# Row maxima of all batches on two banks, the first key rows with a bank and tiles of their own, and the rotations of batches 1 and 2 by ScalarE and GpSimd

## What is computed

```python
# layer 0, per batch
h = layernorm(x) * (1 + ca) + sa                # sa, ca, ga, ... from silu(c) @ wmod
qkv = h @ w_qkv.T                               # 16 heads, head size 8
q, k = rope(q), rope(k)                         # t * cos + rotated(t) * sin
x = x + ga * (softmax(q @ k.T) @ v) @ w_out.T   # 16 heads, 512 x 512 scores each
h = layernorm(x) * (1 + cb) + sb
x = x + gb * top2_of_8_experts(h)               # silu(h w0) * (h w1), then wo
# layer 1, per batch
x = x + ga * gated_unit(layernorm(x) ...)       # hidden, q/k similarity over channels, output
x = x + gb * one_expert(layernorm(x) ...)       # 128 -> 512 -> 128, gelu
```

## Time and profile before

| | |
|---|---|
| median of 3 runs | 981.61 us (981.26 to 983.02) |
| the profiled execution's own time | 982.85 us |
| its span, first to last instruction | 981.0 us |
| mean granted TensorE clock | 0.916 of full speed |
| TensorE busy | 831.7 us (85%) |
| VectorE busy | 696.9 us (71%) |
| ScalarE busy | 579.7 us (59%) |
| GpSimd busy | 461.6 us (47%) |

### The profile page before, as it was taken

The page is one execution under the profiler, slowest core; times in us unless marked ns, Lnnn a source line. Parts: engine busy times, 40 slices in busy tenths (PEclk is TensorE's granted clock), DMA queues, the critical chain, the costliest instruction groups (busy, mean ns, idle before and its releaser), DMA issues. The chain is left out here.

```text
span 981.0 us, 15587 instructions
## 1 busy us (share of the span) xinstructions
PE 831.7 (85%) x4972; PEld 449.9 (46%) x4972; DVE 696.9 (71%) x1454; ACT 579.7 (59%) x923; POOL 461.6 (47%) x607
## 2 busy tenths in 40 slices
PE   4788888998789978998899989988899888799586
PEld 3222232544245515654464544634564557376353
DVE  6888786688678756788678658847877435577574
ACT  2256676575567466866686668546857864443252
POOL 0152144025458535573747367383645763663201
PEclk9558889999899979999999989989999999889688
DMA  7524344354824354446073613680156045010001
GB/s 207 164 92 99 73 99 164 86 161 130 208 52 148 122 165 92 113 123 192 25 214 95 202 28 114 182 247 17 42 179 198 25 147 180 24 39 19 1 12 38
DMA packets 97063, 110.77 MB, mean 113 GB/s; under 512 B 14191, under 2 KB 76783, under 8 KB 95616
## 3 DMA queue, kind: packets, MB, share of 16 engines
q1 hardware_dynamic: 92954, 102.06, 36.6%
q0 software_dynamic: 3584, 7.35, 2.6%
q10 hardware_dynamic: 444, 0.36, 0.1%
HBM read 84.06 MB, written 26.26 MB: 112 GB/s over the span
## 5 line engine op out<-in xcount | busy, mean ns | idle before, releaser
L1459 ACT ACTIVATE probs<-scores 128x1024 f32<-128x1024 f32 x256 | 262.0, 1024 | 116.0 <-PE scores L1077 84.8
L1772 DVE TENSOR_REDUCE negmax<-scores_for_max 128x2 f32<-128x1024 f32 x192 | 234.3, 1220 | 59.0 <-PE scores_for_max L1052 45.8
L1087 PE MATMUL weighted_values<-probs,vaug 128*32 128x512 f32 x1024 | 147.6, 653 | 1.1 <-ACT probs L1459 1.1
L1149 PE MATMUL expert_units<-xt,ring 128*128 128x128 f32 x840 | 122.7, 289 | 13.4 <-DVE mu L1949 5.6
L1077 PE MATMUL scores<-qs,ks 51*128 51x512 bf16 x512 | 106.0, 407 | 32.3 <-ACT probs L1459 27.9
L1149 PEld LDWEIGHTS expert_units<-xt,ring 128*128 128x128 f32 x840 | 105.2, 195 | 56.3 <-issue 47.6
L1052 PE MATMUL scores_for_max<-ks,qs 48*128 48x512 bf16 x384 | 76.8, 396 | 15.8 <-DVE negmax L1772 11.3
L2222 POOL DMA_INDIRECT xs_d<-xbn,rowpos x56 | 55.6, 994 | 50.2 <-DVE rowpos L1905 35.4
L2233 POOL DMA_INDIRECT y<-ys_d,rowpos x56 | 55.4, 989 | 37.9 <-DMA ys_d<-slot_rows 21.4
L1077 PEld LDWEIGHTS scores<-qs,ks 51*128 51x128 bf16 x512 | 25.5, 94 | 103.2 <-ACT probs L1459 64.2
L1768 DVE TENSOR_REDUCE negmax<-scores_for_max 128x1 f32<-128x512 f32 x86 | 56.4, 682 | 7.5 <-PE scores_for_max L1046 3.6
(11 more groups left out here) (325 smaller groups left out, 1666.3 us busy)
## 6 DMA issues: line engine op xcount, KB each, us to landing
ring<-in_experts SPq DMA_DIRECT2D x113, 384.0 KB, 5.2
slot_rows<-xs_d SPq DMA_DIRECT2D x7, 960.0 KB
parts_d<-parts SPq DMA_DIRECT2D x15, 384.0 KB, 2.6
qs<-parts_d SPq DMA_DIRECT2D x14, 384.0 KB
ks<-parts_d SPq DMA_DIRECT2D x14, 384.0 KB
ys_d<-slot_rows SPq DMA_DIRECT2D x21, 256.0 KB
w<-in_L_ffn_w SPq DMA_DIRECT2D x16, 256.0 KB
parts_d<-parts SPq DMA_DIRECT2D x15, 256.0 KB, 2.9
```

The costliest lines, as they stand in the source:

```text
L1087: last = nc.tensor.matmul(pv[32 * j:32 * j + 32, :], vaug[:, kt, PAIRS * (j // 2) + GP * g + j % 2, :], probs[:, kt % 2, j % 2, j // 2, :] ...
L1149: last = nc.tensor.matmul(dst[:, at], ring[:, q % RING, j, first + f * P:first + (f + 1) * P], xt[:, q % 2, at], start=True, stop=True)
L1459: nc.scalar.activation(probs[:, kt % 2, j, :, :].rearrange("p m s -> p (m s)"), se[:, :], ACT.Exp)\
L1772: V.tensor_reduce(negmax[:, g % 2, :, n], sm[:, :].rearrange("p (m s) -> p m s", m=2), AX, ALU.max, negate=True)\
```

## The change

1. The three banks of batches 0 and 1 go. All batches take the pair of banks and one reduction of 1024 columns. Only the first group of batch 0 alternates between the pair `sm` and the pair `se`, which no exponential uses yet.
2. In batch 0 the k projection has its own bank (`m0`, shared_ab), and its rotation, sum and remainder have tiles of their own (`uz`, `u2`, `nt3`), so that it waits for nothing of q. The modulation products that used `m0` go to `wp`. Several VectorE steps of the start wait until the last part of k is written.
3. `p_store` is a step for each part, sent when that part is written, and `p_stack` a step for q and one for k.
4. In batches 1 and 2 (`COPIED`) VectorE doesn't rotate. ScalarE copies the projection out of PSUM into `uz` and, with the halves exchanged, into `u2` (step `turn`, 3 ACTIVATEs), and GpSimd multiplies by `cosT` and `sinT` and subtracts (3 operations in place of its 1).
5. The whole slot table is new.

```diff
-EARLY = 2
+COPIED = (1, 2)
...
-        def max_unit(b, g, n, m):
-            return 2 * GROUPS * GP * NT * b + 2 * (GP * NT * g + n) + m
-
-        def max_unit_bank(u):
-            return (sm[:, 0:512], sm[:, 512:1024], wp[:, :])[u % 3]
+        def max_bank(b, g, n):
+
+            return se if b == 0 and g == 0 and n % 2 else sm
...
+        def proj_bank(b, n):
+            return m0 if (b, n) == (0, 1) else m1
+
+        def turned(b, n):
+
+            return (uz, u2, nt3) if (b, n) == (0, 1) else (rot1, rot2, rem)
...
-                if b < EARLY:
-                    for m in range(2):
-                        at, u = slice(HALF * m, HALF * m + STACK), max_unit(b, g, n, m)
-                        after(pe, "a_max", 0, u - 2)
-                        nc.tensor.matmul(max_unit_bank(u), qs[at, b % 2, p, t * P:(t + 1) * P], ks[at, b % 2, p, :],
-                                         start=True, stop=True).then_inc(sig["a_smf"], 1)
-                    return
-                after(pe, "a_max", b, 8 * g + n)
+                if b == 0 and g == 0:
+                    if n == 1:
+                        pe.wait_ge(s_m1, SM_COPIED)
+                    after(pe, "a_max", b, max(n - 1, 0))
+                else:
+                    after(pe, "a_max", b, 8 * g + n)
...
+            def turn(b, n):
+                if b not in COPIED:
+                    return
+                after(act, "p_proj", b, n + 1)
+                after(act, "p_sum", b, n)
+                nc.scalar.activation(uz[:, :], m1[:, :], ACT.Copy)
+                nc.scalar.activation(u2[0:HALF, :], m1[HALF:P, :], ACT.Copy)
+                nc.scalar.activation(u2[HALF:P, :], m1[0:HALF, :], ACT.Copy).then_inc(sig["p_rot"], 1)
...
             def mod_second(b, part):
 
                 if b == 0 and part == 0:
+                    after(dve, "p_part2", b, 2)
...
             def rot(b, n, k):
+                if b in COPIED:
+                    return
...
+                if b in COPIED:
+                    pool.wait_ge(s_rope, 16 * N_ROPE)
+                    first = 4 * COPIED.index(b) + 2 * n
+                    G.tensor_tensor(uz[:, :], uz[:, :], cosT[:, :], ALU.mult).then_inc(sig["p_mul"], 1)
+                    G.tensor_tensor(u2[:, :], u2[:, :], sinT[:, :], ALU.mult).then_inc(sig["p_mul"], 1)
+                    pool.wait_ge(sig["p_mul"], first + 2)
+                    G.tensor_tensor(rem[:, :], uz[:, :], u2[:, :], ALU.subtract).then_inc(sig["p_sum"], 1)
+                    return
...
-        ("P", "xT"): dict(pe=(86, 137, 160, 278, 389, 512, 671, 929)),
+        ("P", "xT"): dict(pe=(86, 153, 178, 278, 386, 513, 659, 902)),
```

More of the change, by code:

```diff
@@ L829, in p_stack @@
[L829 to L841 removed]
+                n = k if which else PARTS - 1 - k
```

468 lines of the change are left out of this document (232 added, 236 removed), and 118 rows, old and new, of the table SLOTS.

## The result

The changed kernel takes 992.33 us (median of 3 runs, 988.69 to 1000.0) where the kernel before takes 981.61: ratio 1.0117, 95% interval 1.0062 to 1.0171. It is slower by 10.7 us; the forecast was 4.9 us slower. The profiled execution is the longest of the three, with 1000.0 us and a span of 997.9; it took 7.7 us more than the median, so part of what stands in its trace is that execution's own.

A forecast was written before the change was run, and what follows sets the result against it. TensorE was held to bound the kernel from 165.5 us on, with no engine always full before; the change acts on the first 165 us. -2.8 + 3 + 5.1 - 0.4 = +4.9 us, by the median 986.5 us; range 974 to 992 us.

The forecast's parts named there:

- The pace: Attention units at full clock: reductions 1.71 us apart with 0.49 us idle for the refill, in place of 1.51 us.
- P of batch 1: Preparation of batch 1, moved behind the first maxima on TensorE, between exponentials: 6.4 us at half clock, costed at +3 us.
- rival c: First 165 us: a further clock loss or a full ScalarE makes it slower, 992 us; chance 0.11 together with late stack.
- The first reduction starts at about 35.4 us: 2.8 us earlier: Start of batch 0: shorter VectorE chain and batch 1's work moved behind the maxima, 35.4 in place of 38.18 us.
- The stack doesn't hold it: Start of batch 0: the stack DMAs of k land by 34.2 us, before the first reduction, with 1.2 us cover.
- One pair of banks: +5.1 us: Row maxima of batches 0 and 1 share one pair: 0.20 us a unit at full clock, bounds 0 to 31 us.
- Rotations "at nothing": Batches 1 and 2: VectorE loses 8.2 us of products, ScalarE gains 12 copies hidden in the refills; costed at nothing.
- theory C: Expectation set for Run 4: VectorE's freed 8.2 us were worth their time, 995 to 1000 us.
- 3.2 early: First exponential of batch 0: 2.8 us from the start and 0.4 us from no longer standing behind a projection.
- 3 + 0.8 + 1.6: Batch 0 losses: 3 us for batch 1's preparation, then bank-pair losses of 0.8 from 69.9 us and 1.6 from 104 us.
- The new slot table also reshuffles later batches ... I cost that at nothing: Order of later batches: moved by at most some 30 places of 1,250; nothing in the sum, put into the range.
- the sign of being wrong: From 165 us on: the prediction is wrong if that time changes by more than the start did.

The follow-up runs named there:

- run 6: Changed kernel with its start mended in three places (small constants behind v, first group sent ahead, gated weights behind the first partial maxima): 970.58 us, ratio 1.0096.
- run 5: Changed kernel again, unaltered, on the chip of the next three experiments: 972.35 us, ratio 1.0123 to the kernel before.
- run 12: Changed kernel with the old order from about 840 us on and the start mended in its three places: 976.62 us, ratio 1.0132.
- run 9: Changed kernel in its own order up to about 840 us, from there in the order of the kernel before: 979.3 us, ratio 1.0172.
- run 18: Changed kernel with the start mended in three places and the old order of the steps behind the transposes of step C of batch 7: 1000.29 us, ratio 1.0215.
- run 17: Changed kernel again, unaltered, beside the kernel with both ends mended: 1007.09 us, ratio 1.0278 to the kernel before.
- run 10: Kernel before in its own order up to about 840 us, from there in the changed kernel's order: 971.42 us, ratio 1.0087.
- run 1: Kernel before, own order, with the row maxima of batches 0 and 1 on one pair of banks instead of three single banks: 975.95 us, ratio 1.0168.
- run 8: Kernel before, own order, row maxima on one pair of banks, but on two pairs in turn in batch 0's first group: 972.55 us, ratio 1.0122.
- run 7: Changed kernel, in its order, with the row maxima of batches 0 and 1 on three single banks again: 971.27 us, ratio 1.0115.
- Run 4: Changed kernel with the rotations of batches 1 and 2 on VectorE again: 976.53 us, ratio 1.0179.
- run 2: Changed kernel in its own order up to about 167 us, from there in the order of the kernel before: 978.93 us, ratio 1.0188.
- run 13: Kernel before, unaltered, run for its trace: 978.27 us, ratio 0.998.
- run 16: Kernel before with the changed kernel's order of the last 60 us alone: 985.19 us, ratio 1.0033.
- run 3: Kernel before, own code and order up to batch 1's last row maximum, from there in the changed kernel's order: 972.27 us, ratio 1.0121.
- run 11: Kernel before with the changed kernel's order only between about 167 and 840 us: 978.24 us, ratio 1.0153.
- run 15: Changed kernel with the old order of the last 60 us alone: 997.45 us, ratio 1.0156.
- run 14: Changed kernel with the old order from about 840 us on for TensorE, VectorE and ScalarE, but its own on GpSimd: 1004.1 us, ratio 1.0192.

## Why the prediction was wrong

**What held.** The pace: 1.72 us a unit with 0.49 us of refill, and the last exponential of batch 0 at 120.24 us ("about 120 us"; the terms themselves give 118.9). The 3 us for P of batch 1 were not tested alone. That the early clock would cost more (rival c) is wrong for the first profiled run, which has more of the full clock up to 104 us than before. The measured 992.33 us is that rival's 992, by luck: up to 104 us the clock was not lost, and no run tested for a full ScalarE.

**"The first reduction starts at about 35.4 us: 2.8 us earlier".** It came at 38.14. The length of VectorE's chain was right (9.85 us for 9.7); the step failed because it took the start of that chain and the landing of the stack from the order of before. "The stack doesn't hold it", with 1.2 us of cover, is the sentence that fell: k lands 6 us after its issue, behind two large transfers that the changed code sends first, and the small constants ahead of v cost 2.3 us. Mended, the reduction is at 35.53 us, so the size was right for a kernel that does not have these waits. What it is worth at the end stays open: 1.8 us (run 6 to 5) and 2.7 us (run 12 to 9) by medians within the noise, with the lead gone by 110 us in both pairs of traces, and 2.9 us kept at 200 us in the third pair (run 18 to 17).

**"One pair of banks: +5.1 us".** In the old order it is about twice that: 1.0122, some 11 us, with 4.9 us at the end of batch 0 and 7 to 8 at 150 us. In the new order taking the pair away gives 1.1 us in the total, within the noise, and 2.4 to 2.8 us up to 155 us, before a stretch at a lower clock. So the price depends on the order: between exponentials a refill costs 0.2 us, as the term had it; maxima one behind another leave TensorE idle for 1.1 to 1.4 us each, and the clock is lower besides (run 10). The rule of the Trainium skill that the prediction weighed (Perfetto Trace Analysis, Optimizing Tensor Performance (Matmuls): independent groups rotate through banks) is borne out in the old order (runs 1 and 8); in the new one (run 7) the trace agrees with it up to 155 us, and the total doesn't show it. The term should have counted how many maxima stand bare; it used one share for all 64.

**Rotations "at nothing".** Not shown either way. Run 4, without the move, has the number of theory C, and is 7.1 us behind run 5 from 90 us on, a part of it by the clock. So the move may be worth some us, which the sum didn't have.

Errors of opposite sign nearly met by the end of batch 0: at the first exponential 0.9 us late where 3.2 early was forecast, and from there to the last exponential of batch 0 a loss of 2.6 us where the terms had 5.4 (3 + 0.8 + 1.6). Together 3.5 us late, 2.2 by the terms. That this came out near is luck.

**"The new slot table also reshuffles later batches ... I cost that at nothing".** This is the step that failed and that carries the number. Behind batch 1 lie 10.9 of the 16.9 us of the first pair of traces, and 15.2 of the 24.6 of the second (the first changed trace is 7.7 us above its median, so there the share behind batch 1 is uncertain). The term was nothing, with no reason but the number of places; and the sign of being wrong that the prediction named, a time from 165 us on that changes by more than the start did, came true. From the last exponential of batch 1 to the end of the trace, over all traces (us):

| order behind 167 us | chips where the kernel before takes 960 to 963 | chips where it takes 978 to 982 |
|---|---|---|
| old | 769.8, 770.1, 770.8 (runs 1, 2, 8) | 791.7, 788.6 (before, run 13) |
| old, with the new end | 769.9 (run 10, from 840 us) | 787.5 (run 16, last 60 us) |
| new | 772.4, 774.3, 770.4, 774.4, 769.9 (runs 5, 6, 7, 3, 4) | 802.6, 803.8 (changed, run 17) |
| new, with the old end | 779.5, 777.3, 779.3 (runs 9, 12, 11, from 840 us) | 797.6, 799.9 (runs 15, 18, last 60 us), 801.9 (run 14, from 840 us but for GpSimd) |

So the term at nothing measures -1 to 5 us on chips of the first kind and 11 to 15 (new against the order of before) on the kind on which the forecast stood. What is shown of it: about 5 us in the last 60 us, where the order of 11 steps on TensorE is the cause behind the new middle (from output 6 to output 7 46.6, 46.4 and 46.6 us with it, in the first trace and runs 5 and 17, 41.6 and 41.8 without, in runs 15 and 18; mended with the start 6.8 us together, of which 2.9 are the start's at 200 us). Behind the old middle the same exchange is worth 0.3 us in the traces (run 16), at a better clock, so what these steps cost depends on the rest of the table. That four steps can cost 7.5 us (run 10) shows how wrong "at most some 30 places of 1,250" was as a reason for nothing.

**What stays open.** Why the new order loses the rest on the slower chips is only placed, not explained. Between 200 and 800 us the same instructions in the new order take 25 to 31 us more there than on the other chips (run 5 against the first trace and runs 14, 15, 17 and 18), in the old order 18 to 25 (run 10 against before, 13 and 16). These losses come in good part in steps of 3 to 6 us at which TensorE stands still; the last section has one. They also fit the change costing 1.2% on the chips of one kind and 1.6% to 2.8% in two groups on the other; the first measurement, 1.2% there too, has three runs that spread over 11 us.

No kernel here that has the change beats the kernel before. With both ends mended, run 18, it is still 1.0215 on its chip.

## What to carry to other kernels

A table of slots is a schedule for one kernel: when it is made anew, its differences from the old one are a part of the change like any other, and each place where an instruction now stands behind a later wait (a constant's load, a large transfer, a statistic of the next stage) is to be read from the trace, in the last stages above all, where one batch is left and nothing hides a misplaced product. Price a shared bank by the places where its users stand bare, not by a mean per unit. And two schedules can't be compared by joining halves of them without looking at the seam, nor two traces by where they are level without looking at the clock of both.

## What the runs showed of the hardware

The same instructions take 966.0 us of span on one chip and 1003.4 on another. A window of the changed kernel, run 5, then run 17:

```profile
240.00:262.00 22.00, 18.85 (x140) 7.33 (x138) 15.74 (x23) 15.42 (x20) 11.19 (x15) 1.00 0.67 209
```

```profile
240.00:262.00 22.00, 15.23 (x109) 7.50 (x102) 13.72 (x25) 10.65 (x16) 12.42 (x15) 0.86 0.46 145
```

Where run 5 has the full clock throughout, run 17 has a stretch at half, and it does 78% of the matmuls. More than the clock is in it: TensorE stands still. The same instructions in the first trace of the changed kernel, then in run 5:

```profile
642.61 0.42 DVE L2078 SCALAR_TENSOR_TENSOR x<-shared_pc,x 128x256 f32<-128x256 f32 x1 [6.52 <-remote]
643.18 3.54 PE L1356 MATMUL shared_pc<-w,kq 128*128 128x128 f32 x16 [5.09 <-issue]
```

```profile
625.22 0.42 DVE L2078 SCALAR_TENSOR_TENSOR x<-shared_pc,x 128x256 f32<-128x256 f32 x1 [1.15 <-PE shared_pc L1356]
625.91 1.95 PE L1356 MATMUL shared_pc<-w,kq 128*128 128x128 f32 x16
```

VectorE waits 6.52 us for matmuls that it waits 1.15 us for in run 5, TensorE then has a gap of 5.09 us where run 5 has none, and goes on at half clock (3.54 us in place of 1.95). "remote" means that the profile has no instruction for what ended the wait. Waits so marked stand at 5 to 8 places in each of the eight traces from chips where the kernel before takes 978 to 982 us, in the old order too, and in none of the twelve others; two traces of one kernel have them at the same instructions. What TensorE waits for there no trace shows.

The clock also falls at different places in kernels that are the same so far: from 74 to 112 us run 14 has 0.55 and run 15 0.83, on one chip and with the same head. Run 14 there:

```profile
74.00:112.00 38.00, 33.50 (x134) 7.67 (x134) 18.21 (x19) 24.96 (x36) 20.96 (x24) 0.55 0.40 107
```

and run 15:

```profile
74.00:112.00 38.00, 28.67 (x160) 7.42 (x158) 21.71 (x21) 28.91 (x40) 21.04 (x24) 0.83 0.45 122
```

Between them lie 1.1 us at 74 us and 5.7 at 120, with the same instructions in the same order: about as much as the forecast was for the whole change.
